# Score steps in pairs and one ring of six PSUM banks in a fused attention block

## The reference, cut to what matters

```python
x = L0_attn_x                                  # (8, 1024, 512), float32
xn = layernorm(x)
# attention part: 16 heads of 64, two null keys and values, causal, with a slope per head
q = (layernorm2(xn) @ Wq); k, v = split(xn @ Wkv)
k = concat([nk, k]); v = concat([nv, v])
sim = 8.0 * l2norm(q) * q_scale @ (l2norm(k) * k_scale).T
sim = sim + slope[h] * -abs(j - i);  sim = where(causal, -max, sim)
out = (softmax(sim) @ v) @ Wout
# the second part, as far as the kernel reads its parameters: layernorm(xn) * ln_g + ln_b
return x + out + second_part
```

## Time and profile before

| | us |
|---|---|
| median of 3 runs | 2699.8 (2696.74 to 2699.81) |
| span of the profiled execution | 2696.2 |
| PE busy | 2622.8, 97% of the span |
| DVE busy | 2488.1, 92% |
| ACT busy | 2126.7, 79% |
| POOL busy | 2098.1, 78% |

### The profile page before, as it was taken

The page is one execution under the profiler, slowest core; times in us unless marked ns, Lnnn a source line. Parts: engine busy times, 40 slices in busy tenths (PEclk is TensorE's granted clock), DMA queues, the critical chain, the costliest instruction groups (busy, mean ns, idle before and its releaser), DMA issues.

```text
span 2696.2 us, 84329 instructions
## 1 busy us (share of the span) xinstructions
PE 2622.8 (97%) x31631; PEld 1575.9 (58%) x31631; DVE 2488.1 (92%) x6760; ACT 2126.7 (79%) x3385; POOL 2098.1 (78%) x2438
## 2 busy tenths in 40 slices
PE   5799999999999999999999999999999999999997
PEld 4455565565565565565555565565655665565654
DVE  8999998999999999999999999999998999989986
ACT  5688887888877888877887878787887888877876
POOL 6677887779867788678887788777887778877775
PEclk8899999999999999999999999999999999999999
DMA  5333344434544334333443435433353433544222
GB/s 177 67 63 74 81 102 99 91 71 82 102 100 94 69 87 98 96 87 76 90 107 82 93 75 101 100 95 71 80 107 87 100 74 76 98 100 80 54 59 71
DMA packets 638790, 236.94 MB, mean 88 GB/s; under 512 B 594609, under 2 KB 596657, under 8 KB 638385
## 3 DMA queue, kind: packets, MB, share of 16 engines
q1 hardware_dynamic: 636912, 231.45, 39.6%
q10 hardware_dynamic: 1472, 0.09, 0.0%
HBM read 72.01 MB, written 16.78 MB: 33 GB/s over the span
## 4 chain that ended last, share of the span: by engine, by line
PE 81%; DVE 7%; issue 3%; DMA 2%; POOL 1%; SPq 1%; ACT 1%; DVEq 0%; POOLq 0%; ACTq 0%
PE PS L1259 12%; PE PS L1236 11%; PE PS L1238 10%; PE PS L1237 10%; PE PS L1283 6%; PE PS L1322 6%; PE PS L1326 4%; PE PS L1324 4%; PE PS L1263 4%; PE PS L1349 4%; PE PS L1350 3%; PE PS L1351 3%; DVE PS L1034 3%; DVE AR L1075 1%; PE PS L1294 1%
## 5 line engine op out<-in xcount | busy, mean ns | idle before, releaser
L1034 DVE CUSTOM_DVE_ANT_0 PS<-PS,STR 128x512 f32<-128x512 f32 (+3 forms) x1536 | 822.5, 580 | 121.9 <-PE PS L1283 114.9
L598 ACT ACTIVATE AR<-PS,SC 128x1024 f32<-128x1024 f32 (+1 forms) x640 | 655.1, 1024 | 143.5 <-PE PS L1294 75.7
L1236 PE MATMUL PS<-WH,XT 128*128 128x388 f16 x2048 | 676.7, 330 | 22.5 <-DVE AR L1047 13.5
L1237 PE MATMUL PS<-WL,XT 128*128 128x388 f16 x2048 | 673.9, 329 | 0.0
L1238 PE MATMUL PS<-WH,XT 128*128 128x388 f16 x2048 | 673.7, 329 | 0.0
L602 ACT ACTIVATE AR<-AR 128x1024 f16<-128x1024 f32 (+1 forms) x640 | 622.0, 972 | 20.3
L803 POOL TENSOR_TENSOR RN<-SS,HALF 128x8 f32<-128x8 f32 x256 | 453.6, 1772 | 182.7 <-DVE SS L1122 181.6
L1075 DVE TENSOR_TENSOR AR<-AR 128x768 f16<-128x768 f32 (+1 forms) x448 | 503.4, 1134 | 11.8 <-ACT AR L602 11.7
L1259 PE MATMUL PS<-AR 64*128 64x512 f16 (+3 forms) x4608 | 495.4, 324 | 9.1 <-ACT AR L598 8.9
L1322 PE MATMUL PS<-AR 128*128 128x66 f16 x4608 | 472.3, 195 | 1.8 <-DVE AR L1075 0.8
L1324 PE MATMUL PS<-AR 128*128 128x64 f16 x4608 | 468.8, 192 | 0.0
(11 more groups left out here) (227 smaller groups left out, 5197.2 us busy)
## 6 DMA issues: line engine op xcount, KB each, us to landing
XW<-in_L_attn_x SPq DMA_DIRECT2D x112, 256.0 KB, 3.0
XB<-in_L_attn_x SPq DMA_DIRECT2D x64, 256.0 KB, 3.0
out<-ACC SPq DMA_DIRECT2D x64, 256.0 KB, 2.3
ACC<-in_L_attn_x SPq DMA_DIRECT2D x56, 256.0 KB, 3.0
AR<-QKB SPq DMA_TRANSPOSE x512, 2.5
AR<-in_L_attn_Wkv SPq DMA_DIRECT2D x2, 1536.0 KB, 12.7
ACC<-in_L_attn_x SPq DMA_DIRECT2D x2, 1024.0 KB, 7.1
AR<-in_L_attn_Wout SPq DMA_DIRECT2D x1, 2048.0 KB, 8.4
```

Source lines behind the costliest of these rows:

```text
L598: e.activation(PR[:, n % 2, :, 0:wide], SB[:, :, 0:wide], ACT.Exp, scale=SIG).then_inc(s_p, 1)
L1034: e.tensor_tensor_reduce(out=r[:, 0:n], in0=r[:, 0:n], in1=ST[:, u % 2, h, o:o + n], scale=1.0, scalar=LOW, op0=ALU.add, op1=ALU.max, accu ...
L1236: e.matmul(to, XT[:, k, xs], WH[:, k, p, :], start=k == 0, stop=False)
L1237: e.matmul(to, XT[:, k, xs], WL[:, k, p, :], start=False, stop=False)
```

## The change

- The ring has six banks, 0 to 5, and score steps take theirs from it: `take_pair` gives a step two neighbouring banks, at the pair that is expected to be free first. `AV` moves to banks 6 and 7. A score step waits with `bank_free` for the readers of its two banks; a bank whose last owner was a score step is free when that step's exponential is done. The wait for the exponential of the step before goes.
- `W_SCORE` puts steps in pairs into one slot: 0 and 1, 2 and 3, 4 and 5, 6 and 7, 8 and 9. The cast to float16 has a table of its own, `W_CAST`, behind the exponentials. `PR` keeps two buffers and `PH`, `PL` three.
- Twelve pieces become ten groups: (0,0) with (2,0), and (4,1) with (6,1), 128 + 384 columns, lie side by side in one bank. Their matmuls and maxima stay as many and as wide.
- PE's order within a slot is WOT, pieces, scores with their masks, nvp, value, op, proj.
- The wait for nvp (`s_nv2`) ahead of a unit half's first value step goes; both run on PE.
- `SL` is 50, and all slot tables are new.

```diff
-BANKS = 4
-SL = 48
+BANKS = 6
+SL = 50
+GROUPS = [[(0, 0), (2, 0)], [(3, 0)], [(1, 0)], [(4, 0)], [(5, 0)], [(4, 1), (6, 1)], [(6, 0)], [(5, 1)], [(7, 0)], [(7, 1)]]
-W_PIECE = [47, 53, 56, 59, 66, 68, 69, 77, 79, 82, 83, 86]
-W_SCORE = [88, 96, 105, 108, 111, 115, 118, 126, 130, 133]
-W_PLOW = [94, 100, 101, 105, 108, 115, 122, 125, 131, 135]
-W_VALUE = [108, 109, 110, 116, 124, 127, 130, 136, 141, 149]
-W_NVP = [105, 115]
-W_OP = [121, 121, 138, 149, 160, 160, 167, 170]
-W_PROJ = [z for z in [7, 10, 17, 22, 26, 31, 37, 43] for k in range(KC)]
-W_VL = [3, 7, 16, 21, 24, 27, 40, 42]
+W_PIECE = [54, 54, 64, 69, 70, 79, 79, 89, 94, 94]
+W_MAX = [56, 56, 63, 69, 70, 78, 78, 81, 90, 91]
+W_SCORE = [97, 97, 112, 112, 115, 115, 126, 126, 139, 139]
+W_CAST = [102, 102, 112, 114, 120, 123, 126, 128, 141, 141]
+W_PLOW = [107, 107, 113, 114, 117, 125, 128, 129, 148, 148]
+W_VALUE = [113, 113, 117, 123, 127, 137, 142, 147, 148, 148]
+W_NVP = [112, 121]
+W_OP = [141, 144, 144, 152, 173, 191, 195, 208]
+W_ADD = [137, 146, 148, 155, 174, 188, 192, 209]
+W_PROJ = [z for z in [5, 6, 16, 20, 28, 37, 38, 45] for k in range(KC)]
+W_VL = [7, 8, 18, 23, 29, 30, 37, 51]
-HOLD = [2.0, 2.1, 2.0, 6.7]
+HOLD = [10.5, 10.8, 11.3, 11.9, 11.1]
-W_LATD = [-313, -246, -231, -193, -187, -179, -171, -128, -96, -89, -73, -68, -67, 17, 19, 20]
-W_XF0 = [-177, -170]
-W_WOS = [-194]
-W_VND = [-28]
-W_WOM = [30, 40, 41]
-W_WOT = [46, 53]
+W_LATD = [-322, -304, -267, -229, -222, -204, -200, -184, -159, -141, -111, -99, -66, -55, -8, 42]
+W_XF0 = [-303, -57]
+W_WOS = [-363]
+W_VND = [13]
+W_WOM = [-46, -4, 24]
+W_WOT = [7, 22]
...
+    def take_pair(slot, u, m):
+        i = min(range(BANKS - 1), key=lambda z: (max(read[z], read[z + 1]), read[z] + read[z + 1]))
+        for h in range(2):
+            who = ("sc", u, 2 * m + h)
+            at[who], before[who] = i + h, last[i + h]
+            last[i + h], read[i + h] = who, slot
...
+            elif what == "sc":
+                e.wait_ge(s_p, NS * u + i // 2 + 1)
...
-                    e.activation(PR[:, n % 2, :, 0:wide], SB[:, :, 0:wide], ACT.Exp, scale=SIG).then_inc(s_p, 1)
+                    e.activation(PR[:, n % 2, :, 0:wide], PS[:, low:low + 2, 0:wide], ACT.Exp, scale=SIG).then_inc(s_p, 1)
+                for u, m in due(s, W_CAST):
+                    n = NS * u + m
+                    wide = width(m)
                     w.wait_ge(s_p, n + 1)
...
-                    w.wait_ge(s_p, n)
+                    low = BANK["sc", u, 2 * m]
+                    bank_free(w, "sc", u, 2 * m)
+                    bank_free(w, "sc", u, 2 * m + 1)
...
-                    if blocks[0][0] == 0:
-                        w.wait_ge(s_nv2, 2 * u + qc + 1)
```

More of the change, by code:

```diff
@@ L116, in due, with pieces @@
+def pieces(g):
+    out, at = [], 0
+    done = 2 * sum(len(z) for z in GROUPS[:g])
+    for qt, c in GROUPS[g]:
+        n = min(512, P * (qt + 1) - 512 * c)
+        out.append((qt, c, at, n, done))
+        at += n
+        done += 2
+    return out
 def due(slot, when, units=NU, period=SL):
@@ L155, in ring_order @@
             take(s + HOLD[1], "s", u, 2 * i + 1)
+        for u, m in due(s, W_SCORE):
+            take_pair(s + HOLD[4], u, m)
         for u, t in due_op(s, W_OP):
@@ L331, in rb @@
         def rb(*who):
[L332 removed]
+            return PS[:, BANK[who], :]
         def bank_free(e, *who):
@@ L1242, in _ @@
             for s in SLOTS:
+                for _, i in due(s, W_WOT, 1, BL):
+                    if i == 0:
+                        w.wait_ge(s_wo, 1)
+                        e.transpose(PS[0:1, 6, 0:P], AM[:, 5:6], IDF[:, :]).then_inc(s_won, 1)
+                    else:
+                        w.wait_ge(s_wop, 1)
+                        e.matmul(PS[:, 6, P:P + 1], ONE[0:1, :], M8[0:1, :], start=True, stop=True).then_inc(s_won, 1)
+                for u, i in due(s, W_PIECE):
+                    bank_free(w, "s", u, 2 * i)
+                    bank_free(w, "s", u, 2 * i + 1)
+                    for qt, c, at, n, done in pieces(i):
+                        for g in range(qt // 2 + 1):
+                            w.wait_ge(s_kq[g], 32 * (u + 1))
+                        for h in range(2):
+                            hs = slice(64 * h, 64 * h + 64)
+                            e.matmul(rb("s", u, 2 * i + h)[:, at:at + n], KQ[hs, u % 2, QH, P * qt:P * qt + P],
+                                     KQ[hs, u % 2, KH, 512 * c:512 * c + n], start=not at, stop=True,
+                                     skip_group_check=True).then_inc(s_s, 1)
                 for u, m in due(s, W_SCORE):
                     qc, blocks = STEPS[m]
-                    n = NS * u + m
-                    w.wait_ge(s_p, n)
+                    low = BANK["sc", u, 2 * m]
+                    bank_free(w, "sc", u, 2 * m)
+                    bank_free(w, "sc", u, 2 * m + 1)
                     for g in range(max(2 * qc + 1, blocks[-1][0] // 2) + 1):
@@ L1262, in _ @@
                             hs = slice(64 * h, 64 * h + 64)
-                            ins = e.matmul(SB[:, h, to], AL[hs, kt - 4 * qc + 4, :], CT[hs, u % 2, qs], start=False,
+                            ins = e.matmul(PS[:, low + h, to], AL[hs, kt - 4 * qc + 4, :], CT[hs, u % 2, qs], start=False,
                                            stop=kt < 4 * qc, skip_group_check=True)
@@ L1293, in _ @@
                                     to = slice(off + 64 * a, off + 64 * a + 64)
-                                    ins = e.matmul(SB[:, h, to], TRI[hs, a, :], IDB[hs, hs], start=False, stop=True,
+                                    ins = e.matmul(PS[:, low + h, to], TRI[hs, a, :], IDB[hs, hs], start=False, stop=True,
                                                    skip_group_check=True)
```

137 lines of the change are left out of this document (56 added, 81 removed).

## The result

The changed kernel takes **2912.3 us** (median of 4 runs, 2910.5 to 2914.9) against 2699.6 (4 runs): ratio **1.0787**, 95% interval 1.0772 to 1.0802. It is 213 us slower, where 17 us faster had been forecast.

A forecast was written before the change was run, and what follows sets the result against it. PE's own work was taken as the bound, at 40.54 us a unit with DVE next. Banks -19, prologue +4 and tail -2 summed to -17 us, so 2683 us from 2699.8, with an eight-in-ten range of 2664 to 2716.

The forecast's parts named there:

- Work: Whole kernel: no instruction added or taken away, so DVE's 37.7 us and PE's 38.0 a unit stay.
- PE's work: Middle units: PE's matmuls and tile changes sum to 39.9 of 40.54 us a unit, leaving 0.6 of waits.
- Changes of tile: PE's switches between 128-row and 64-row matmuls: twenty a unit before and after, 0 us.
- Banks: PSUM ring in the middle: a slacker ring removes half of PE's 0.6 us waits, -0.3 a unit, -19 us.
- The chain from score to value: Exponentials, casts and low halves between score and value: one microsecond left before piece 4, so 0 us.
- Start: Prologue: DVE idles about 5 us for Wout ahead of its early reduction; +4 us, from +2 to +8.
- no difference: Clock in the prologue: the longer stop restarts PE at a lower clock as the old one did.
- Tail: End of the kernel after the last projection: -2 us, from -5 to +4.
- DVE takes over: Rival, middle: bursts of maxima make DVE decide, 3.2 us idle a unit, +27 us, 2727 us; chance 0.20.
- slower: Measured time slower by more than about 0.2% (5.4 us); chance 0.19.

The follow-up runs named there:

- e10b: Changed kernel, POOL's low half only writing zeros once, and DVE's low half made for one head only from unit 1 on; 2711.0 us, ratio 1.0035.
- e9: Changed kernel, with DVE making the low half of the probabilities for one head only from unit 1 on; 2814.8 us, ratio 1.0427.
- e9c: Kernel before, with DVE making the low half of the probabilities for one head only from unit 1 on (control); 2691.5 us, ratio 0.9972.
- e13: Changed kernel, POOL's low half replaced by writing zeros twice and a bit, about as long as the real step but without reading; 2819.7 us, ratio 1.0441.
- e13c: Kernel before, POOL's low half replaced by writing zeros twice and a bit, without reading (control); 2703.8 us, ratio 1.0014.
- e10: Changed kernel, POOL's low half replaced by writing zeros once, short and without reading; 2756.7 us, ratio 1.0204.
- e10c: Kernel before, POOL's low half replaced by writing zeros once, short and without reading (control); 2713.4 us, ratio 1.0045.
- e1: Changed kernel's code and six-bank ring, but the old slot tables and single score steps; 2763.3 us, ratio 1.0235 against the kernel before.
- e11: Six-bank ring with old slot tables and single steps, read times chosen to keep a bank's users furthest apart on PE; 2843.8 us, ratio 1.0526.
- e12: Changed kernel with the old slots for Wout's mean, its transposes and scalings and the null values; 2905.0 us, ratio 1.0760.
- e8: Kernel before with one more DVE reduction behind each low half of q and k, 2.7 us a unit; 2761.0 us, ratio 1.0228.
- m1: Separate kernel repeating three DVE forms alone, then beside POOL's low half, power and writes; the difference took 692 ns alone, 1022 beside the low half.

## Why the prediction was wrong

**Where the 213 us go.** Going down from after: POOL's reading of SBUF 93, POOL's duration 63, relief of DVE 46, and 11 that remain between e10b and before, nearly all at the start (unit 8 is 14 late there, the stretch from unit 56 to the end takes 392.0 against 392.1). The terms depend on the order in which they are taken away: DVE's relief is worth 98 us when the collisions are still there (e9) and 46 when they are gone.

The last two are not work that the change added, since the kernel before has the same. What the new order makes of it shows when both kernels get the same edit. Their distance is 213 us as they are, 123 with DVE relieved (e9, e9c), 116 with POOL writing as long (e13, e13c) and 43 with POOL writing once (e10, e10c). In the traces of that last pair 19 of the 43 lie ahead of unit 8 and 21 in the 48 units behind it; what makes the 21 is not shown, only that they go with 3.2 us less DVE work.

**Work (the step that failed).** "DVE's 37.7 us and PE's 38.0 stay": the term for DVE's work was put at nothing. The instructions stayed, their durations didn't: +3.06 us a unit, where a unit got 3.24 longer. I took busy time in the profile for work, although it holds the waits for POOL too. Before's own trace had it: LO there lasts 826 ns on average and 656 at its shortest, and 150 us of DVE's 2488 were such waits. A new order shifts which DVE and POOL instructions overlap, and I never listed those pairs. In the old tables only 20 us of waits end with POOL's PLOW, in the new ones 173. Taking POOL's reading away gave 93 us back (e13).

**PE's work.** The sum of 39.9 us prices a pair of masks at 0.053, while the prediction's own reading of the masks at 1204.24 takes 0.03. With 0.03 throughout it is 39.5, and PE waited 1.0 us a unit in the kernel before, not 0.6; the later count says 0.98. So there was more to win than forecast, and none of it came.

**Changes of tile.** Counted in both traces over units 8 to 56: twenty a unit, before and after; no gain from pairs. Right.

**Banks (failed, and not by the port alone).** -0.3 us a unit was forecast since users of a bank stand further apart. With all burdens off (e10b) the pace is 40.52, not 40.25. The ring alone, under the old tables, with e1's read times, costs 1.0 us a unit. The step compared PE's distance with the length of one maximum or exponential, and named "the wait in that engine's queue" without putting a number on it. e11 shows what that is worth: distances improved by this very reckoning, and 81 us lost to VL standing late in DVE's queue.

**The chain from score to value (failed in size).** "One microsecond is left: 0 us" was worked out for steps 2 to 5 with PLOW on DVE at 1.01 us, the row of 768 columns, though step 3 has 1024 (1.29). POOL's PLOW of steps 0, 4 and 7 takes 2.15: ACT L623, which was to wait for neither, waits 42.3 us for POOL and 64.6 for DVE's PLOW, against 5.2 and 1.1 in the kernel before. e10 takes POOL's part away (4.0), leaves DVE's (59.6), and is 63 us below e13. The wait on POOL, which the prediction didn't price, mattered; how much of the 63 goes by late exponentials and how much by late values isn't parted.

**Start.** Right in kind: DVE's gap ahead of the reduction was forecast at about 5 us and is 3.90, the first reading of a projected tile (L1073, the counterpart of the row at 70.38) at 76.3 and is at 75.75, PE "8 us behind" and waits 21.8 instead of 13.5.

```profile
70.66 4.42 DVE L1171 TENSOR_REDUCE OT<-AR 128x1 f32<-128x4096 f32 x1 [3.90 <-DMA AR<-in_L_attn_Wout]
...
75.75 0.27 DVE L1073 TENSOR_TENSOR QKB<-PS,BQF 128x132 f32<-128x132 f32 x1
```

The tables that I had looked at make 2 to 3 us (e12; forecast 4, from 2 to 8). The whole start in e10b is 14: other tables had moved as well, and the clock, for which "no difference" was said, is 0.76 from 46.8 to 134 instead of 0.85.

**Tail.** From unit 56 on e10b, at the old pace, has 0 where -2 was forecast: within its range. From the last projection to the end it takes 75.0 us instead of 69.5 (limit set: 73), but its last projections end that much sooner. In the changed kernel it is 81.

**The rivals.** "DVE takes over" had the sign and PE's waits for maxima and VL, but not the mechanism: it let DVE decide above 2.5 us of idle time, 3.2 at worst, with work fixed, hence 2727. DVE idles 2.82, and its busy time grew. The bursts of maxima are still in e10, which takes 41.26, so they can't make more than a small part of the loss; e10's own distance from the old pace, with DVE idling 3.00, is about what this rival described, and isn't excluded. A chance of 0.19 for "slower" rested on PE being at 99% in the old order. That says how well the old tables fit, not that new ones will. In the kernel before, 2.7 us more DVE work cost 0.9 us a unit (e8), so DVE's idle time didn't take up such an addition, and the highest rival stood at 2727 us.

## What to carry to other kernels

Before a change of order, list for each DVE instruction with two SBUF inputs which POOL instruction that reads SBUF it will overlap, and compare mean with shortest duration of each form: in this kernel the difference was waiting, and it moved with the order. Price a hand-over by when the reader's queue gets to it, on every engine that can make the step, not by the reader's duration. And an order in which PE, DVE, ACT and POOL stand above 75% each is a fit, not a bound: new tables start from the assumption that it is lost.

## What the runs showed of the hardware

- A DVE difference of 512 columns with both inputs in SBUF takes 692 ns alone and beside POOL's writes; beside POOL reading 1024 columns the first took 2643, those behind it 978 to 982, 1022 on average (m1). POOL's 2.14 us became 3.11 when DVE was first.
- Instructions of 8 columns are held up too: 194 ns at the 5th percentile, 254 on average in the old order, 447 in the new one (L1096, now L1123).
- A power of 8 columns on POOL takes 2093 ns, and DVE's difference beside it 693 (m1): the length of this POOL instruction doesn't tell how long it keeps the port.
- Busy time in the profile contains such waits: 150 us of DVE's 2488 before, 341 of 2679 after, with 6760 instructions in both.
- A change between 128-row and 64-row matmuls takes 0.096 us, twenty times a unit in both kernels.
